# Sparse feed-forward kernel on one core: the first row gather of w1 issued as two gathers of half rows

## The reference

```python
rates = relu(inputs) * 0.001
c = initial_state[:, None, :] + cumsum(rates, axis=1)
fl = floor(c); spikes = (fl - shifted(fl)) / 0.001
# x_flat = spikes as [2048, 256]
probs = softmax(x_flat @ router_w.T); top_v, top_i = top_k(probs, 2); top_v /= sum(top_v)
for k in range(2):
    # tokens put in expert buffers of C = 640 rows by their order
    h = gelu(einsum('ech,ehf->ecf', expert_in, w1), approximate=False)   # w1: [8, 256, 1024]
    y = einsum('ecf,efh->ech', h, w2)                                    # w2: [8, 1024, 256]
    out = out + tok * (gate * keep)[:, None]
return x + out
```

## Time and profile before

| what | value |
|---|---|
| median of 3 runs | 61.05 us (60.81 to 61.36) |
| time of the profiled execution | 60.7 us |
| its span in the trace | 59.0 us, 1243 instructions |
| PE busy | 50.2 us (85%) |
| DVE busy | 38.8 us (66%) |
| ACT busy | 32.0 us (54%) |
| POOL busy | 22.1 us (38%) |
| mean granted TensorE clock | 0.978 |

### The profile page before, as it was taken

How to read it: one execution, slowest core, us unless ns; L and a number is a source line. 1 busy time by engine, 2 the same in 40 slices (tenths; PEclk the granted TensorE clock), 3 DMA queues, 4 the chain that set the end, 5 groups by cost and what they waited for, 6 DMA issues and landing times.

```text
span 59.0 us, 1243 instructions
## 1 busy us (share of the span) xinstructions
PE 50.2 (85%) x407; PEld 30.4 (52%) x407; DVE 38.8 (66%) x152; ACT 32.0 (54%) x57; POOL 22.1 (38%) x66
## 2 busy tenths in 40 slices
PE   2999999999997899989899999999999999980000
PEld 0325365765432444343876699765966666550000
DVE  3299999975969747999898787699952250342000
ACT  0499899881596867370054867999996020000000
POOL 5799999767130900647776000000000000005700
PEclk9999999999999999999999999999999999999965
DMA  0499999999999999546688518999999999100220
GB/s 0 87 341 282 350 356 345 365 348 349 348 343 336 349 347 357 154 62 181 203 314 304 186 19 242 381 296 376 364 345 376 379 385 348 64 0 0 93 63 11
DMA packets 13545, 14.82 MB, mean 251 GB/s; under 512 B 648, under 2 KB 13040, under 8 KB 13536
## 3 DMA queue, kind: packets, MB, share of 16 engines
q1 hardware_dynamic: 12608, 12.62, 65.9%
q0 software_dynamic: 816, 2.01, 10.9%
q10 hardware_dynamic: 112, 0.07, 0.6%
HBM read 13.08 MB, written 2.36 MB: 262 GB/s over the span
## 4 chain that ended last, share of the span: by engine, by line
PE 51%; DMA 14%; DVE 12%; issue 9%; POOL 3%; SPq 3%; ACT 1%; DVEq 0%; POOLq 0%
PE bank L782 24%; DMA x_sb<-in_x_dram 8%; PE bank L762 7%; DMA w_got<-in_L_ffn_w_dram,w_index 7%; PE bank L568 6%; PE bank L745 5%; POOL out_dram L558 3%; DVE floors L1068 3%; DVE x_lo L1059 3%; SPq L408 2%; PE bank L798 2%; DVE floors L1275 1%; PE bank L799 1%; PE bank L792 1%; ACT x_hi L884 1%
## 5 line engine op out<-in xcount | busy, mean ns | idle before, releaser
L568 PE MATMUL bank<-ones_b 128*128 128x512 bf16 x49 | 14.3, 421 | 1.2 <-POOL ones_b L444 1.2
L782 PE MATMUL bank<-w_sb,spare_sb 128*64 128x256 f32 x128 | 14.7, 382 | 0.0
L782 PEld LDWEIGHTS bank<-w_sb,spare_sb 128*64 128x64 f32 x128 | 8.8, 137 | 4.5
L558 POOL DMA_INDIRECT out_dram<-floors,out_index x2 | 2.0, 1016 | 21.9 <-DVE floors L1275 21.6
L568 PEld LDWEIGHTS bank<-ones_b 128*128 128x128 bf16 x49 | 4.3, 104 | 5.4 <-issue 2.0
L539 POOL DMA_INDIRECT w_got<-in_L_ffn_w_dram,w_index x4 | 4.1, 1018 | 4.9 <-ACT w_got L873 3.5
L1159 DVE TENSOR_SCALAR rate<-bank,pair_gate 128x256 f32<-128x256 f32 x4 | 1.9, 482 | 4.8 <-PE bank L782 4.8
L1059 DVE SCALAR_TENSOR_TENSOR x_lo<-x_sb,x_hi 128x512 fp32r<-128x512 f32 x7 | 4.6, 693 | 0.1
L884 ACT ACTIVATE x_hi<-x_sb 128x512 fp32r<-128x512 f32 x7 | 4.3, 627 | 0.4 <-DMA x_sb<-in_x_dram 0.2
L762 PE MATMUL bank<-ev_pair,w_got 128*128 128x128 f32 x32 | 4.1, 281 | 0.3 <-DMA w_got<-in_L_ffn_w_dram,w_index 0.3
L873 ACT COPY w_got<-zero 128x1024 f32<-128x1024 f32 x4 | 4.2, 1040 | 0.0
(11 more groups left out here) (237 smaller groups left out, 99.6 us busy)
## 6 DMA issues: line engine op xcount, KB each, us to landing
w_sb<-in_L_ffn_w_dram SPq DMA_DIRECT2D x8, 1024.0 KB, 10.5
x_sb<-in_x_dram SPq DMA_DIRECT2D x8, 256.0 KB, 4.6
out_dram<-x_sb SPq DMA_DIRECT2D x1, 2048.0 KB, 14.1
cond<-in_cond_dram ACTq DMA_DIRECT2D x2, 32.0 KB, 2.1
w_got<-in_L_ffn_w_dram,w_index POOLq DMA_INDIRECT x4
cond<-in_cond_dram SPq DMA_DIRECT2D x1, 32.0 KB, 1.9
x_rows<-in_x_dram,out_index POOLq DMA_INDIRECT x2
out_dram<-floors,out_index POOLq DMA_INDIRECT x2, 3.0
```

The costliest lines, as they stand in the source:

```text
L558: g.indirect_dma_start(out=out_rows[:, :], out_offset=bass.IndirectOffsetOnAxis(ap=out_index[:, t:t + 1], axis=0), in_=ffn_out[:, t, :], i ...
L568: nc.tensor.matmul(bank[2][:, 0:4 * P], ones_b[:, :], ones_b[:, :].unsqueeze(1).to_broadcast([P, 4, P]), start=True, stop=True)
L782: mm = nc.tensor.matmul(Y[d % 2][at, :], hT[:, d % 2, f, at], w2_sb[:, 2 * d + side, f, :], start=(f == 0), stop=(f == FC - 1))
```

## The change

The first gather becomes two gathers of 128 half rows (2 KB each), the first columns 0 to 511 of `w1_got[:, 0, :]`, then columns 512 to 1023. The view `w1_half_rows` numbers half rows, so the row number is doubled, and `ev_info` gets two more columns (3 and 4) with doubled values, MI = 5. DVE computes two columns of row numbers for group 0 in place of one. The first half lands on a semaphore of its own, `w1_first_in`; the second on `w1_in[0]`. PE waits for the first before chunk 0 and for the second before chunk 4. `WARM[3]` is 3 in place of 6.

```diff
-    MI = 3
+    MI = 5
...
-    WARM = (4, 4, 4, 6)
+    WARM = (4, 4, 4, 3)
...
+    w1_half_rows = w1.rearrange("e h (s f) -> (e h s) f", s=2)
...
-        w1_index = sb("w1_index", [P, D], I32)
+        w1_index = sb("w1_index", [P, D + 1], I32)
...
-        MASKS = 26
+        MASKS = 28
...
+            g.memset(ev_info[:, :, 0:E:2, 4], -2.0 * FAR).then_inc(masks, 1)
+            g.memset(ev_info[:, :, 1:E:2, 4], 2.0 * H - 2.0 * FAR).then_inc(masks, 1)
...
+            g.tensor_scalar(ev_info[:, :, :, 3], info[:, :, 0].unsqueeze(2).to_broadcast([P, ST, E]), 2.0 / FINE, 2.0,
+                            ALU.mult, ALU.add).then_inc(channels_set, 1)
+
+            def gather_first(half, landed):
+
+                pool.wait_ge(indexed, half + 1)
+                at = D if half else 0
+                g.indirect_dma_start(
+                    out=w1_got[:, 0, half * (FFN // 2):(half + 1) * (FFN // 2)], out_offset=None, in_=w1_half_rows[:, :],
+                    in_offset=bass.IndirectOffsetOnAxis(ap=w1_index[:, at:at + 1], axis=0),
+                    bounds_check=last_w1_half, oob_is_err=False, compute_op=ALU.bypass).then_inc(landed, 16)
 
             def gather(d):
                 pool.wait_ge(cleared, d + 1)
-                pool.wait_ge(indexed, d + 1)
+                pool.wait_ge(indexed, d + 2)
...
-            for d in range(D):
+            pool.wait_ge(cleared, 1)
+            gather_first(0, w1_first_in)
+            gather_first(1, w1_in[0])
+            for d in range(1, D):
                 gather(d)
...
-                    pe.wait_ge(channels_set, 1)
+                    pe.wait_ge(channels_set, 2)
...
-                pe.wait_ge(w1_in[d], 16)
                 pe.wait_ge(map_out, d + 1)
                 for half in range(2):
+                    if d == 0 and half == 0:
+                        pe.wait_ge(w1_first_in, 16)
+                    elif d == 0 or half == 0:
+                        pe.wait_ge(w1_in[d], 16)
...
                 dve.wait_ge(mapped, d + 1)
-                v.tensor_scalar(w1_index[:, d:d + 1], MAP[d][:, 0:1], MAP[d][:, 1:2], 2 * d * H - 1 + FAR, ALU.add, ALU.add).then_inc(indexed, 1)
+                if d == 0:
+                    for half, at in enumerate((0, D)):
+                        v.tensor_scalar(w1_index[:, at:at + 1], MAP[0][:, 3:4], MAP[0][:, 4:5], 2 * (FAR - 1) + half,
+                                        ALU.add, ALU.add).then_inc(indexed, 1)
+                else:
+                    v.tensor_scalar(w1_index[:, d:d + 1], MAP[d][:, 0:1], MAP[d][:, 1:2], 2 * d * H - 1 + FAR, ALU.add, ALU.add).then_inc(indexed, 1)
```

More of the change, by code:

```diff
@@ L323, in adaln_ffn_kernel @@
         indexed = sem("indexed")
+        w1_first_in = sem("w1_first_in")
         pair_mm = sem("pair_mm")
@@ L442, in _ @@
             last_w1_row = g.to_reg(E * H - 1)
+            last_w1_half = g.to_reg(2 * E * H - 1)
             g.memset(ones_b[:, :], 1.0).then_inc(ones_set, 1)
```

## The result

The changed kernel takes 61.22 us (median of 22 runs, 60.64 to 62.16), the kernel before 61.01 us (22 runs). The ratio on record is 1.0086, 95% interval 1.0062 to 1.011, which would be 0.5 us; the two medians are only 0.21 us apart. So the change costs 0.2 to 0.5 us, less than the 1% that the prediction calls no change, and 60.75 was forecast, a gain. Ratios here compare fast executions, those within 1.5% of their kernel's fastest, but the traces of e4, e9 to e11, e13, e14 and e18 come from slower ones, so I compare stretches counted from the first map product and not their ends.

The account below looks back on a forecast made before the run. The first gather, then almost only PE, was taken to bound the kernel. Half rows save 0.6, less 1.30 of POOL, plus 0.99 hidden PE work: gain about 0.3, median 61.05 to 60.75 us, range 60.3 to 61.45.

Parts of the forecast that it names:

- (a): First half row gather: 3.95 us from issue to landing shrinks by 0.6, landing at 27.44; PE starts 0.27 later, at 27.71.
- the 0.4 that stands beside it: Alternative saving for the first half gather, from the DMA page's fixed 2.0 us plus bytes; total gain then 0.1.
- (b): Second half row gather: 1.30 us of POOL behind the first, lands at 28.74; PE starts its second half at 29.01.
- s - 0.31: Gain at project(0): s, the half rows' saving (0.6), minus 1.30 of POOL plus 0.99 of PE work; 0.29 us.
- Fewer warming products: Three removed before hidden(0), so PE is free by about 27.4; needed for the first half's gain, worth 0 itself.
- the clock: PE's granted clock stays at 1.00 despite 0.3 us gaps, cost 0; rival that it falls, time 66, chance 0.01.
- the DVE instruction: Added second column of row numbers on DVE, up to 0.23 us, taken up by idle time; cost 0, else 0.2.
- the MAP columns: Map products on PE with 5 columns in place of 3; cost 0.
- Group 2's rows ... 0.80 later is 32.97 at the worst ... Just covered.: Later gathers 0.80 us later; group 2's parts ready about 35.7 and 36.4, PE asking at 35.9; no cost.
- the shift of the later gathers binds: Rival: later gathers or w2 delay the copy, first scatter waits; 61.15 at 0.8 us beyond the shift, chance 0.08.
- The slower rival, (b) late in its queue: Second half lands 0.2 to 0.5 us later, at 28.94 to 29.24; 60.95 with 0.5; chance 0.23.
- 60.25: Best time of the faster rival: second half's start-up hides behind the first, gain 0.6 to 0.8; chance 0.14.

Follow-up runs that it names:

- e4: Kernel before plus only the change's additions ahead of the gather (columns, memsets, tensor_scalar, second row-number column), one whole gather, six warming products; ratio 1.002 (0.998 to 1.006).
- e9: The kernel before, unchanged, run again for a second trace; ratio 1.001 (0.995 to 1.007).
- e11: The changed kernel with only the row limit's register (to_reg) moved behind POOL's masks; ratio to the kernel before 1.001 (0.997 to 1.005).
- e13: The changed kernel, unchanged, run again on another chip; ratio to the kernel before 1.042 (1.035 to 1.048).
- e14: The changed kernel with group 2's gather issued ahead of group 1's; ratio to the kernel before 1.032 (1.024 to 1.040).
- e18: The changed kernel, unchanged, run beside the kernel before with an empty gather; ratio to the kernel before 1.024 (1.017 to 1.030).
- e2: The kernel before with group 2's gather issued ahead of group 1's; ratio 0.996 (0.992 to 1.000).
- e3: The kernel before with one more gather behind the first that moves no rows; ratio 1.004 (0.999 to 1.008).
- e17: The kernel before with one more gather behind the first that moves no rows, run again; ratio 1.045 (1.039 to 1.051).
- e6: The changed kernel with group 2's gather ahead of group 1's and the row limit's register moved behind POOL's masks; ratio to the kernel before 1.007 (1.003 to 1.011).
- e5: The kernel before with the gathers of groups 2 and 3 exchanged, nothing added; ratio 1.031 (1.024 to 1.037).
- e8: The changed kernel with PE waiting for both halves before its first product; ratio to the kernel before 1.024 (1.017 to 1.030).
- e15: The kernel before with group 2's gather issued ahead of group 1's, run again; ratio 1.001 (0.996 to 1.006).

## Why the prediction was wrong

- *(a) saves 0.6 of 3.95, and PE starts 0.27 after a landing.* The 3.3 us were right (3.3 to 3.5 in other traces), the two terms beside it were not. A gather raises its semaphore 16 times as it lands, and the first trace of before holds only 11 of the first gather's 16; 28.04 is the last of these, not the landing. In the traces that hold all 16 a whole first gather took 4.13 to 4.34 (e2, e3, e4, e9), and PE began 0.04 to 0.05 after the landing where it was free (e2, e3, e9). So a half saves some 0.8 to 1.0, not 0.6 (nor the 0.4 that stands beside it), and the hand-over is 0.05, not 0.27. The two errors partly cancel, and that the sum came so near is in part luck.
- *(b) is 1.30 behind and the gain is s - 0.31 = 0.29.* Near: 1.4 behind, PE waits 0.3 between the halves, and project(0) starts 0.2 to 0.4 earlier, counted from the map, in the traces of the change and of the changed order without late gelus.
- *Fewer warming products, the clock, the DVE instruction, the MAP columns: 0.* No run shows a cost of them for certain, though e4 leaves room for 0.6%; the granted clock was 1.00 throughout 22 to 52 us in the change and in e17. Not tried alone was the number of warming products.
- ***The failed step: "Group 2's rows ... 0.80 later is 32.97 at the worst ... Just covered."*** They landed at 33.75. POOL's shift itself was as I said, 0.82 counted from the map. What failed is the cover. I took it from one execution, in which group 2's rows were on their way for 4.9 us at most; the traces that show it with the gathers in their old order (the change's, e3, e4, e9 to e11) have 5.2 to 5.7, and e9, the same kernel, has no cover. And even by my own rows it wasn't covered: L745 starts at 36.02 before, 0.29 earlier is 35.73 and not 35.9, DVE's first part ends at 34.27 + 0.70 = 34.97, 0.80 later is 35.77, and PE starts 0.25 after it (36.57 and 36.82 in the chain above). That makes a wait of 0.29, which I put at nothing. The sign turned there: 0.38 gained at project(0) became 0.48 lost by project(1). In the measured ratio a share of the additions' own cost stays open (e4).
- *The rival "the shift of the later gathers binds".* Right mechanism, wrong place: I put it at the copy and the first scatter and gave it 0.08. The scatter was still released by DVE. That its price, 0.4, is near the 0.48 seen is chance: it was worked out for another wait.
- *The slower rival, (b) late in its queue.* Didn't happen: (b) took as long as (a).
- Two sums in the rivals were off. With (b) 0.5 late the loss is 0.5 - 0.29, so the time is 61.25 and not 60.95, which belongs to 0.2 late. And with (a) landing at 27.44 PE's first half is through at 28.70, so no start of (b) can gain more than 0.60: 60.45, not 60.25.
- Late signals were in no rival. They don't explain the 1.0086, as far as one trace shows: it has none. They go with the ratios of 1.02 to 1.045 on three of the five chips (e6, with one of them, is at 1.007; e5, with none, at 1.031).

No version is clearly better than the kernel before. The change itself gave 1.009, 0.996, 1.042 and 1.024. The halves with group 2's gather first gave 0.998 and 0.990 on two chips, and 1.032 on a third.

## What to carry to other kernels

Splitting a transfer to start its consumer earlier adds an issue step to a serial queue, and everything behind it in that queue pays what the queue's idle time doesn't take up (here 0.82 us of 1.30); look up first who waits for the last one that still has little slack. Slack read from one execution is a bound only if the event that ended the wait is the transfer itself: here ACT's own late gelu stood in front and hid where the rows landed. A landing read from a trace should be checked for missing increments. A hand-over between engines (0.25 us from DVE to PE here) belongs in the sum. And a gain of some tenths of a microsecond should be run on more than one chip.

## What the runs showed of the hardware

In the first trace of the kernel before the third gelu of group 0 already starts 1.3 us after its product's end (30.36 by the earlier trace rows), as this row of ACT's timeline shows:

```profile
31.67 0.38 ACT L927 ACTIVATE spare_sb<-bank 128x256 f32<-128x256 f32 x1 [1.29 <-PE bank L762]
```

Gelus were late only between about 30 and 35.5 us, by 0.9 to 3.2 us, while POOL's gathers were under way. Two in a row are often 1.46 to 1.51 us apart (32.79 and 34.27 in e8), or 2.84 to 2.88 (32.13 and 35.01 in e13). All other gelus of group 0 start within 0.3 us of their product's end or of the gelu before. In e17 the semaphore that ACT waits for is recorded as rising at 32.61, ACT starts at 32.63, and the product's row ends at 29.42. So ACT isn't the late one; whether the product (the ends of matmuls are modelled) or its signal is, the traces don't tell.

The records of semaphores differ in the same traces. In the first trace of before, in e5 to e8 and in e13 to e18 not one of POOL's w1 gathers has all its 16 increments on record; in all other traces each has. That holds for e5 and e15 too, whose gelus are on time. So it goes with the chip, and late gelus were seen where such a chip met one gather more, and once (1.3 us) without it, in the row above. Why stays open.
